# Layer norms taken in two halves of the tokens, and two norms in a row folded into one, in a four-layer cross-attention kernel

## The reference

```python
x = x + _L0_xattn_ref(_layernorm(x, axis=-1), ctx_1024, ...)   # 16 heads of 8
x = x + _L0_ffn_ref(_layernorm(x, axis=-1), ...)               # ternary weights, 8-bit activations
x = x + _L1_xattn_ref(ctx_1024, _layernorm(x, axis=-1), ...)   # latents, normed again inside
x = x + _L1_ffn_ref(_layernorm(x, axis=-1), ...)               # mixture of 8 experts
x = x + _L2_xattn_ref(_layernorm(x, axis=-1), ctx_1024, ...)   # 16 heads of 64, normed inside and at its end
x = x + _L2_ffn_ref(_layernorm(x, axis=-1), ...)               # mixture of 8 experts
x = x + _L3_xattn_ref(_layernorm(x, axis=-1), ctx_1024, ...)   # 16 heads of 8
x = x + _L3_ffn_ref(_layernorm(x, axis=-1), ...)               # ternary weights
```

## Time and profile before

| | |
|---|---|
| median of 3 runs | 2422.94 us (2419.05 to 2427.33) |
| the profiled execution's own time | 2423.16 us |
| its span, first to last instruction | 2421.4 us |
| mean granted clock of TensorE | 0.931 |
| busy: PE, DVE, ACT, POOL | 2160.7, 1462.5, 1190.6, 608.3 us |
| powers of the norms on POOL (L122, L1114, L1117) | 11 |

### The profile page before, as it was taken

The page is one execution under the profiler, slowest core; times in us unless marked ns, Lnnn a source line. Parts: engine busy times, 40 slices in busy tenths (PEclk is TensorE's granted clock), DMA queues, the critical chain, the costliest instruction groups (busy, mean ns, idle before and its releaser), DMA issues. The chain is left out here.

```text
span 2421.4 us, 49106 instructions
## 1 busy us (share of the span) xinstructions
PE 2160.7 (89%) x19446; PEld 1584.6 (65%) x19446; DVE 1462.5 (60%) x3180; ACT 1190.6 (49%) x2227; POOL 608.3 (25%) x231
## 2 busy tenths in 40 slices
PE   6999999537999688799999999999995889999995
PEld 3666667427888544467777777777773456776773
DVE  5677677568887354645544554455425567777774
ACT  5777776304666221234444444444430266766761
POOL 6656553004656100600000000000000063343400
PEclk8999999758999789799999999999997889999996
DMA  6444443022432001200000010000000154444420
GB/s 165 137 141 129 136 137 102 14 56 80 137 114 73 18 26 39 68 20 17 19 31 17 17 28 22 17 17 17 1 1 9 51 156 124 130 141 124 116 64 17
DMA packets 87008, 165.17 MB, mean 68 GB/s; under 512 B 40352, under 2 KB 48560, under 8 KB 86528
## 3 DMA queue, kind: packets, MB, share of 16 engines
q1 hardware_dynamic: 86784, 162.06, 23.3%
HBM read 81.73 MB, written 0.46 MB: 34 GB/s over the span
## 5 line engine op out<-in xcount | busy, mean ns | idle before, releaser
L1534 PEld LDWEIGHTS L2ps<-L2values,L2probsT 125*128 125x128 f32 (+1 forms) x2688 | 317.5, 192 | 50.6 <-issue 49.6
L1515 PE MATMUL L2ps<-L2keys,L2qz 128*128 128x501 f32 x672 | 339.5, 589 | 0.9 <-DVE L2out_bias L1778 0.9
L1534 PE MATMUL L2ps<-L2values,L2probsT 125*128 125x128 f32 (+1 forms) x2688 | 318.4, 275 | 0.0
L1731 DVE CUSTOM_DVE_ANT_0 L2work<-L2ps,L2maskadd,L2big 128x1503 f32<-128x1503 f32 x112 | 199.7, 1783 | 162.8 <-PE L2ps L1515 162.8
L122 POOL TENSOR_TENSOR rstd<-mv,half_neg 112x8 f32<-112x8 f32 x9 | 16.8, 1865 | 1021.5 <-DVE mv L138 1021.5
L1529 PEld LDWEIGHTS L2ps<-const,L2work 128*126 128x126 f32 x1344 | 163.8, 140 | 116.7 <-issue 65.0
L647 ACT ACTIVATE L3probsT<-L3ps 128x448 f32<-128x448 f32 x384 | 191.8, 547 | 84.9 <-PE L3ps L504 84.7
L647 ACT ACTIVATE L0probsT<-L0ps 128x448 f32<-128x448 f32 x384 | 193.0, 550 | 67.4 <-PE L0ps L504 67.3
L1529 PE MATMUL L2ps<-const,L2work 128*126 128x128 f32 x1344 | 202.2, 273 | 2.0 <-ACT L2work L1655 1.2
L785 DVE TENSOR_REDUCE L0partmax<-L0ps 112x1 f32<-112x1000 f32 x128 | 153.3, 1197 | 72.9 <-PE L0ps L477 72.6
L785 DVE TENSOR_REDUCE L3partmax<-L3ps 112x1 f32<-112x1000 f32 x128 | 153.3, 1197 | 64.0 <-PE L3ps L477 63.6
(11 more groups left out here) (459 smaller groups left out, 4195.2 us busy)
## 6 DMA issues: line engine op xcount, KB each, us to landing
L0key_stack<-L0key_parts SPq DMA_DIRECT2D x192, 187.5 KB
L3key_stack<-L3key_parts SPq DMA_DIRECT2D x192, 187.5 KB
L0ctxT<-in_ctxT SPq DMA_DIRECT2D x16, 750.0 KB, 4.3
L1raw<-in_ctx SPq DMA_DIRECT2D x16, 750.0 KB
L1rawT<-in_ctxT SPq DMA_DIRECT2D x16, 750.0 KB, 6.2
L2raw<-in_ctx SPq DMA_DIRECT2D x16, 750.0 KB
L3ctxT<-in_ctxT SPq DMA_DIRECT2D x16, 750.0 KB, 4.5
L1fw<-in_L_w SPq DMA_DIRECT2D x16, 256.0 KB, 2.8
```

The lines of the kernel that those rows point to most:

```text
L1515: last = nc.tensor.matmul(PS[:, 3 * (m % 2) + c, 0:NPR], tile_rows(m), KT[:, m // RT % 2, 500 * c:500 * c + NPR], start=True, stop=True)
L1534: last = nc.tensor.matmul(PS[:, bank, 0:P], PT[0:keys_in(c), i % 2, c, :], V[0:keys_in(c), i // RT % 2, c, :], start=c == 0, stop=c == NCH ...
L1731: nc.vector.tensor_tensor_reduce(SM[:, m % 2, :].rearrange("p (c n) -> p c n", c=3), PS[:, 3 * (m % 2):3 * (m % 2) + 3, 0:NPR], MA[:, m // ...
```

## The change

The four helpers work on two halves of 448 tokens (four tiles each), with one signal for each half; POOL takes two powers of four columns in the place of one of eight. Statistics of both halves come first, then `meanwhile(0)`, then both halves of `xn`, then `meanwhile(1)`. With two constants there is one pass: for a variance v the two norms multiply up to (x - mean) times (v (1 + e1) + e0 e1) to the power -1/2, so the addition becomes a multiplication and an addition, and the second statistics, the second power and the second normalising are gone.

```diff
 def ln_pe(pe, k, s, ps, feature_major=True, stream=None):
...
+    for h in range(2):
+        for t in range(4):
+            last = nc.tensor.transpose(ps[0:TT, h, t * P:(t + 1) * P], ...)
+        last.then_inc(s.ln_tok, 1)
...
 def ln_turn(pe, k, s, ps):
-    pe.wait_ge(s.ln_norm, 1)
...
+    for h in range(2):
+        pe.wait_ge(s.ln_norm, h + 1)
+        for t in range(4):
+            last = nc.tensor.transpose(ps[:, 2 + h, t * TT:(t + 1) * TT], k.xn[:, 4 * h + t, :], k.ident[0:TT, 0:TT])
+        last.then_inc(s.ln_feat, 1)
...
+def ln_pool(pool, k, s):
     nc = k.nc
+    for h in range(2):
+        pool.wait_ge(s.ln_var, h + 1)
+        nc.gpsimd.tensor_tensor(k.rstd[:, 4 * h:4 * h + 4], k.mv[:, 4 * h:4 * h + 4, 1], k.half_neg[0:TT, 0:4],
                                 ALU.pow).then_inc(s.ln_rstd, 1)
...
 def ln_dve(dve, k, s, ps, link, eps, scale=None, bias=None, feature_major=True, meanwhile=None):
-    dve.wait_ge(s.ln_tok, 1)
     src = lambda t: ps[0:TT, t // 4, (t % 4) * P:(t % 4 + 1) * P]
-    for n, e in enumerate(eps):
...
+    for h in range(2):
+        tiles = range(4 * h, 4 * h + 4)
+        dve.wait_ge(s.ln_tok, h + 1)
+        for t in tiles:
             last = nc.vector.bn_stats(k.stats[:, t, :], src(t))
         link(last)
+        for t in tiles:
             last = nc.vector.bn_aggr(k.mv[:, t, :], k.stats[:, t, :])
         link(last)
+        var = k.mv[:, 4 * h:4 * h + 4, 1]
+        if len(eps) == 1:
+            last = nc.vector.tensor_scalar(var, var, eps[0], None, ALU.add)
+        else:
+            last = nc.vector.tensor_scalar(var, var, 1.0 + eps[1], eps[0] * eps[1], ALU.mult, ALU.add)
+        last.then_inc(s.ln_var, 1)
+    if meanwhile:
+        meanwhile(0)
+    for h in range(2):
+        dve.wait_ge(s.ln_rstd, h + 1)
+        for t in range(4 * h, 4 * h + 4):
             last = nc.vector.tensor_scalar(k.xn[:, t, :], src(t), k.mv[:, t, 0:1], k.rstd[:, t:t + 1],
                                            ALU.subtract, ALU.mult)
...
+        last.then_inc(s.ln_norm, 1)
+    if meanwhile:
+        meanwhile(1)
     if not feature_major:
         return
-    dve.wait_ge(s.ln_feat, 1)
     for h in range(2):
+        dve.wait_ge(s.ln_feat, h + 1)
...
-            pool.wait_ge(s.ln_var, 1)
-            nc.gpsimd.tensor_tensor(k.rstd[:], k.mv[:, :, 1], k.half_neg[0:TT, 0:NTT], ALU.pow).then_inc(s.ln_rstd, 1)
+            ln_pool(pool, k, s)
             deviations(0)
-            pool.wait_ge(s.ln_var, 2)
-            nc.gpsimd.tensor_tensor(k.rstd[:], k.mv[:, :, 1], k.half_neg[0:TT, 0:NTT], ALU.pow).then_inc(s.ln_rstd, 1)
             deviations(1)
```

More of the change, by code:

```diff
@@ L98, in ln_pe @@
     nc = k.nc
[L99 to L102, removed]
+    for h in range(2):
+        for t in range(4):
+            last = nc.tensor.transpose(ps[0:TT, h, t * P:(t + 1) * P],
+                                       (k.xT if stream is None else stream)[:, h * HALF + t * TT:h * HALF + (t + 1) * TT], k.ident)
+        last.then_inc(s.ln_tok, 1)
     if feature_major:
@@ L109, in ln_turn @@
     nc = k.nc
-    pe.wait_ge(s.ln_norm, 1)
[L111 to L117, removed]
+    for h in range(2):
[4 more added lines that the diff above has]
+def ln_pool(pool, k, s):
     nc = k.nc
-    for n in range(len(eps)):
-        pool.wait_ge(s.ln_var, n + 1)
-        nc.gpsimd.tensor_tensor(k.rstd[:], k.mv[:, :, 1], k.half_neg[0:TT, 0:NTT],
+    for h in range(2):
+        pool.wait_ge(s.ln_var, h + 1)
+        nc.gpsimd.tensor_tensor(k.rstd[:, 4 * h:4 * h + 4], k.mv[:, 4 * h:4 * h + 4, 1], k.half_neg[0:TT, 0:4],
                                 ALU.pow).then_inc(s.ln_rstd, 1)
@@ L128, in ln_dve @@
     nc = k.nc
-    dve.wait_ge(s.ln_tok, 1)
     src = lambda t: ps[0:TT, t // 4, (t % 4) * P:(t % 4 + 1) * P]
-    for n, e in enumerate(eps):
-        for t in range(NTT):
+    for h in range(2):
+        tiles = range(4 * h, 4 * h + 4)
+        dve.wait_ge(s.ln_tok, h + 1)
+        for t in tiles:
             last = nc.vector.bn_stats(k.stats[:, t, :], src(t))
         link(last)
-        for t in range(NTT):
+        for t in tiles:
             last = nc.vector.bn_aggr(k.mv[:, t, :], k.stats[:, t, :])
         link(last)
[L138 to L142, removed]
+        var = k.mv[:, 4 * h:4 * h + 4, 1]
[9 more added lines that the diff above has]
+        for t in range(4 * h, 4 * h + 4):
             last = nc.vector.tensor_scalar(k.xn[:, t, :], src(t), k.mv[:, t, 0:1], k.rstd[:, t:t + 1],
                                            ALU.subtract, ALU.mult)
[L145 to L148, removed]
+        last.then_inc(s.ln_norm, 1)
+    if meanwhile:
+        meanwhile(1)
     if not feature_major:
         return
-    dve.wait_ge(s.ln_feat, 1)
     for h in range(2):
+        dve.wait_ge(s.ln_feat, h + 1)
         out, src2 = k.xnT[:, h * HALF:(h + 1) * HALF], ps[:, 2 + h, 0:HALF]
@@ L620, in _ @@
             pool.wait_ge(s.dup_set, 3)
-            ln_pool(pool, k, s, [1e-5])
-            pool.wait_ge(s.ln_rstd, 1)
+            ln_pool(pool, k, s)
+            pool.wait_ge(s.ln_rstd, 2)
             split(0)
@@ L1621, in _ @@
             pool.wait_ge(s.constants, 4)
-            ln_pool(pool, k, s, [1e-5, 1e-6])
+            ln_pool(pool, k, s)
             pool.wait_ge(s.ln_rstd, 2)
@@ L1628, in _ @@
             pool.wait_ge(s.spread, B // 2)
-            ln_pool(pool, k, s2, [1e-6])
+            ln_pool(pool, k, s2)
         @block.scalar
@@ L1916, in _ @@
             ln_dve(dve, k, s, ps, link, [1e-5], feature_major=False)
-            dve.wait_ge(s.ln_norm, 1)
+            dve.wait_ge(s.ln_norm, 2)
             link(nc.vector.tensor_reduce(xs[:, 0, :], k.xn[:], AX.X, ALU.max, apply_absolute_value=True))
```

1 line of the change is left out of this document (added).

## The result

The changed kernel takes **2400.64 us** (median of 5 runs, 2399.28 to 2400.70) against 2421.71 us for the kernel before, timed beside it (5 runs, 2417.03 to 2427.33). The ratio is 0.9908 with a 95% interval of 0.9897 to 0.9919, which leaves no change out: it is faster by 21.1 us, 0.9%. The forecast was 2403.0 us, in a range of 2396 to 2411. The profiled execution took 2400.64 us, with a span of 2398.9 and a mean granted clock of 0.934 (before: 2421.4 and 0.931).

A forecast was written before the change was run, and what follows sets the result against it. PE was taken to bound most of the time, with norms counting where they stand alone at stage starts, engines waiting in turn. Seven norm savings summed to 20.2 us, taking 2423.16 us to 2403.0, range 2396 to 2411.

The forecast's parts named there:

- L0f: Norm of L0f, which has the bare pattern only up to `xn`: 7.02 us becomes 5.76, 1.3 us saved and kept.
- L3a: Start of L3a: nothing gained, since first scores wait for the stack of keys; bounds zero to 0.5 us.
- L1a: Double norm at L1a's start: w_centred copy 2.47 us earlier, no second pass, turn in halves; 3.2 us saved, bounds 0 and 4.6.
- L3f: Bare norm of L3f: 2.7 us saved by halves, nothing from the transposes ahead, which the wait for a transfer hides.
- L1f: Bare norm of L1f: 3.2 us saved, 2.7 from halves and 0.5 from statistics starting after four transposes.
- L2a's end: Bare norm ending L2a: 3.2 us saved, 2.7 from halves and 0.5 from statistics starting after four transposes.
- L2a's start: Double norm at L2a's start: third weight step and L1554 2.48 us earlier, turn in halves 0.6; together 3.0 us saved.
- The bare pattern: Norms of L1f, L2a's end, L2f, L3f, where engines wait in turn: first statistic to last copy 7.56 us against 10.28.
- The clock: TensorE's clock in the four bare turns: left at half clock; full clock would save some 0.4 us each, 1.6 in all.
- the double norms' gain is not kept: Rival: L1a's and L2a's loops, paced by transfer or POOL, wait out the 6.2 us won; 2409.2 us, chance 0.10.
- the halves' powers are dear: Rival: half powers at 3.60 us, past break-even at 2.7, make the kernel slower: 2425.6 to 2429.2 us, chance 0.08.
- DVE waits behind POOL: Rival: L2a's weight steps wait for running context powers, up to 12.5 us; 2409 to 2415.5 us, chance 0.08.

The follow-up runs named there:

- dear powers: Changed kernel with each half power preceded by two more of its size into a spare tile: 2416.47 us, ratio 0.9981 to the kernel before.
- fold only: Kernel before with the two double norms taken as one and no halves: 2417.76 us, ratio 0.9986 to the kernel before.
- Experiment 2: Kernel before and changed kernel, both unedited, each profiled once more: 2419.94 and 2397.67 us.
- experiment 1: Parts apart: kernel before with double norms as one, no halves, 2417.76 us; changed kernel with both double norms put back, 2405.16 us.
- experiment 5: Changed kernel with POOL's L2a context powers held until DVE's last weight step, 2404.8 us, or until its first set of steps, 2397.85 us.
- experiment 4: Changed kernel with three powers of half size in place of each half power, two into a spare tile: 2416.47 us, ratio 0.9981.

## Why the prediction was right, step by step

The forecast's mechanism is what happened, and its sum, 20.2 us, stands against 21.1. That it came so near is in part luck: L0f and L3a were put too low, L1a perhaps too high, and L3f and L1a scatter by more than the 0.9 that is left. By its terms, with the means of the two profiles of the kernel before and the three of the changed one:

| term | predicted | measured |
|---|---|---|
| L1f | 3.2 | 3.1 |
| L2a's end | 3.2 | 3.4 |
| L2f | 3.6 | 3.5 |
| L3f | 2.7 | 3.5 |
| L0f | 1.3 | 1.9 |
| L2a's start | 3.0 | 3.2 |
| L1a | 3.2 | 1.3 (2.4 with all profiles; one code moves by up to 2) |
| L3a | 0 | 1.2 |
| L0a | 0 | not readable |

*The bare pattern* was put at 7.56 us and took 7.30 at L2a's end, 2.97 less than before, and 7.2 in the other three, 2.8 less. I had charged a seam of 0.06 at each group of four; on DVE there is almost none (normalising eight tiles across two waits took 2.63, the same as before). Four transposes of the turn, put at 0.94, took 1.01. The powers were 1.01 and hidden, as said; one power alone in their place costs 9.7 us, the turn in one piece 5.7.

*L3f* was sized rightly, and nearly all of the 0.8 above the term lies behind the norm. From L3f's first statistic to its first large matmul 2.8 us were saved in all three profiles of the changed kernel. What lies behind moves by itself: that matmul group and the last one took 17.08 and 16.22 us together in the two profiles of the kernel before, and 16.42, 15.05 and 16.65 in the three of the changed one.

*L0f* was sized too small. The pattern up to `xn` fell from 6.99 to 5.46, 1.5 rather than 1.3 for the missing seams. The remaining 0.4 lies at the stage's end, where PE waits 2.18 instead of 2.54 us before the next transposes. It waits 2.18 in every kernel made from the changed one, dear powers included, and 2.54 with the fold only, so it came with the change but not from the norm's length; its cause is open.

*L2a's start.* L1556 came 2.3 us earlier behind the first transposes (18.25 us against 20.56, in the means), where 2.5 were worked out, and the stage is 3.2 shorter, where 3.0 were.

*L3a.* The term was nothing, with a bound of 0.5. The first scores came 0.4 us earlier (1957.75 less 1931.69 before, 1939.30 less 1913.66 after), so the queries do feel the norm a little. It isn't the powers that they feel: with one power and with three powers the first scores are as early (25.5 us into the stage). `xnT` is ready 0.4 earlier (11.4 us into the stage against 11.8), by a first copy that no longer waits for the whole turn. The other 0.8 us lie along the loop or at its end and don't simply follow from the early scores: with three powers L3a took 438.76, as before. No run here tells more.

*L1a*'s start followed the working to the letter (`xnT` 3.2 us earlier, the w_centred copy right behind `xn`). Experiment 2 shows that the first two profiles don't contradict it, but not that the whole 3.2 is kept to the stage's end.

*The clock* was left as it is, and so it was: the bare turns still ran at 0.50, after 3.4 to 7.0 us of idle PE.

*The rivals.* That the double norms' gain is not kept fell in experiment 1 for L2a; for L1a 2.4 of 3.4 us are seen to be kept. That the halves' powers are dear fell with the 1.01 us of line L121, and experiment 4 shows that its price was worked out rightly. That DVE waits behind POOL fell in experiment 5. The Trainium skill's page SBUF — State Buffer, section "Who interferes with whom", has the engine that issues second blocked in full. Here the trace doesn't agree for DVE: its two-input steps took 2.27 to 2.28 us with and without a power of 4.16 us running. For POOL it does. The one context power that starts while such a step runs (at 972.78; the step ends 0.94 us later) took 4.96 us, where the median is 4.16, and in the kernel with the powers held, where no step runs beside them, all eight took 4.16. Timeline of the changed kernel, two powers and the step:

```profile
968.65 9.09 POOL L1629 TENSOR_TENSOR L2rs<-L2rs,half_neg 125x24 f32<-125x24 f32 x2
971.45 2.27 DVE L1750 TENSOR_TENSOR L2work<-L2work 64x2032 f32<-64x2032 f32 x1
```

## What to carry to other kernels

A chain of engines that hand one tile set to each other costs the sum of its parts; in two halves it costs little more than its busiest engine plus one last half, as long as the other engine's work on a half is shorter than what the busiest one can do meanwhile. Work out that break-even before the edit: here it was 2.7 us for a power that took 1.0, and at 3.0 the norm was indeed the slower one. Before a microsecond gained or lost in a long stage is explained, profile the same code twice, and compare the stages that repeat; L1a spread over 4 us among eleven profiles with the same start, more than the 3.2 that was looked for in it.

## What had not been expected of the hardware

The half-clock stretches of TensorE move from one execution of the same code to the next: twelve transposes took 1.47 us at a granted clock of 1.00 in one profile of the kernel before and 2.73 at 0.50 in another. That alone moved the stage by 1.3 us. Sixteen matmuls behind a norm took from 7.71 to 9.13 us in kernels that differ only in their norms, and not in the order of the waits ahead.

A two-input DVE step and a POOL power don't hold each other alike. The step that started while a power ran lost nothing (2.27 to 2.28 us); the power that started while a step ran took longer by about what was left of the step: 0.80 us for 0.94, and in the kernel before 1.57 for 1.62.

A POOL power of four columns costs 1.01 us and one of eight 1.64, so two halves cost only 0.4 us more of POOL's time than a whole.
